# A two-layer metaformer kernel on one core: a new table of numbers for the order of the steps on every engine

## The chip, the cores and the metric

One core of a Trainium2 chip runs the whole program. Its engines are TensorE (PE, the matrix engine, with its weight loads shown as PEld), VectorE (DVE), ScalarE (ACT), GpSimd (POOL) and SyncE (SP, which issues the DMA transfers). The metric is the time of one launch on the device in microseconds. Lower is better.

## What is computed

Thirty-two images of 96 channels and 56 x 56 positions go through two layers. Cut to what matters:

```
# layer 0
x = x + conv0(ln_c(x))      # 1x1 expand 96->576, silu, 3x3 depthwise, silu, squeeze-excite gate,
                            # 1x1 project 576->96, batch norm, + its own input
t = tokens(x); t = t + ffn0(ln_t(t))   # 96->384->96, both products on float8 (5 exponent bits) operands
# layer 1
x = x + conv1(ln_c(x))      # 1x1, group norm over the image, gelu, four shifted copies through two
                            # 1x1 weights, gelu of each, their sum, group norm, 1x1
t = tokens(x); t = t + ffn1(ln_t(t))
```

`ln_c` and `ln_t` normalise each position over its 96 channels. A group norm needs the statistics of a whole image before its first output, and so does the squeeze-excite gate.

## The kernel before

Positions are cut into 8 tiles of 392 (`TW`), numbered 0 to 7. Every stage of an image is a **family** of steps, one per tile (or per chunk of 128 channels and tile), and each engine has its part of a family. The names that the text uses:

- `center_a`, `center 0`, `center 1`, `center 2` and `var ...`: a product that takes the mean off (L523, L598), read by ACT twice (L691 copy, L692 square), then products that sum the squares (L511). `rstd_a`, `rstd 0`, `rstd 1`, `rstd 2` (`seed`, L820) on DVE turn a full set of sums into inverse roots; SP stores them to DRAM and fetches them back broadcast to all channels (`fetch ...`); `norm ...` on DVE multiplies (L842, L901, L906).
- `expand k` (L535, ACT L715), `dw k h j` on DVE: chunk k, half h of the image, tap j of nine, one pass over 128 x 1568 numbers each (L856 for tap 0, L859 for the others); `silu2 k h` on ACT (L742). The last 192 channels go through `texp` (L544, ACT L722) and `tconv` (L557, ACT L733) on PE instead.
- `se1`, `se2`, `se3`: the gate (PE L567, L573; ACT L747, L751; DVE L863 to L871). `proj` (L583, L585) needs it; DVE `x1` (L885) reads it.
- `up`, `quant`, `down`, `add`: the feed-forward blocks, 0 and 1 (PE L618, L627; ACT L775, L782, L789; DVE L914, L921, L924).
- `conv1` (L639, ACT L796), `stats` (L929), `gn 0` (DVE L946 to L966, with two tiny products L646), `gelu1` (ACT L804), `shift` (SP, five DMAs per tile from `g` to `shifted`), `combo` (PE L663, 12 products; ACT three gelus, L810), `fold` (L673, ACT L814), `sum` (DVE L979), `gn 1`, `gn_weights`, `conv3` (L682), `x2` (L983).

The order in which each engine meets its steps is written out by hand: `TIMES` holds for every engine and family one number per step. `timetable` adds 10000 per image, and sorts; an engine then executes its steps in that order. The numbers are keys for the sort alone. No step starts by them: each waits on semaphores for what it needs, and what stands behind a waiting step on its engine waits too. Layer 0 of an image, layer 1 of the image before, and the last feed-forward block of the one before that are in work together, so a steady cycle holds one of each step of all families.

`with_banks` shares three PSUM banks (`ring`, `RING = 3`) among the families of `USES_RING` in the order of PE's steps: a product takes the bank whose last reader has the smallest number, and `wait_bank` makes it wait for that reader. So the numbers of ACT and DVE also decide which bank a product gets.

```
bank = min(free, key=lambda b: free[b])
prev = last[bank]
...
free[bank] = read_at[i, reader]
```

ACT holds one set of function tables at a time. Silu (L715, L722, L733, L742, L747) and gelu (L804, L810) are in different sets, copies and squares in either, so an `ACT_TABLE_LOAD` is put ahead of each first silu after a gelu and the other way round.

Of the kernel before, what the change touches and what calls it, by code (L numbers as in the profile page):

```python
# [47 lines left out]
        "load_x": (1832,), "rstd_a": (4902,), "fetch_a": (4931, 5374, 5857, 5900, 6400, 6627, 6900, 6929),  # L48
        "save_s": (5677, 6677, 6723, 6855, 7082, 7091, 7815, 8098), "texp 0": (8799, 9304, 10303, 10366),
        "texp 1": (11310, 11671, 11721, 12321), "texp 2": (13348, 13418, 13488, 13551),  # L50
        "fetch_s": (17458, 17933, 18453, 18458, 18703, 18742, 19029, 19049), "rstd 0": (20616,),
        "fetch 0": (20784, 20831, 20837, 20843, 21157, 21301, 21302, 21694), "rstd 1": (22328,),
        "fetch 1": (23260, 23290, 23343, 23381, 23422, 23460, 23664, 24595),
        "shift": (24665, 24876, 24982, 25058, 25721, 25722, 26264, 26463), "rstd 2": (28520,),
        "fetch 2": (28558, 28645, 28683, 28721, 29544, 30077, 30293, 30355),
        "store": (30260, 30746, 30809, 30936, 31085, 31161, 31687, 31821)},
# [1145 lines left out]
```

## Time and profile before

| | us |
|---|---|
| runs of the kernel | 6851.56, 6858.68, 6858.77 (median 6858.68) |
| the profiled execution: its time | 6854.27 |
| its span from first to last instruction | 6852.4 |
| busy in it: PE, DVE, ACT, POOL | 5730.9 (84%), 5543.4 (81%), 4409.0 (64%), 452.6 (7%) |
| mean granted TensorE clock (of full speed) | 0.959 |

The times around the span are 1.9 us. The shares are averages over 32 cycles (one for each image in steady work), and a cycle has stretches of different kinds, so a share says little until it is read stretch by stretch.

### The profile page before, as it was taken

The numbers are of one execution on the slowest core, as the hardware profiler recorded it, in microseconds if no ns is written. First come the engines' busy times: TensorE is split into PE (matmuls) and PEld (weight loads), VectorE is DVE, ScalarE is ACT, GpSimd is POOL, SyncE is SP. The second block draws the span as 40 slices with busy tenths as digits, with TensorE's granted clock in tenths as the row PEclk, the third lists the DMA queues.
The fourth block names the chain that finished last, engine by engine and source line by source line (L and its number), as shares of the span: only waits on it lengthen the run. The fifth ranks groups of instructions, "written<-read, shape, count | busy, mean of one in ns | idle before, by whom it ended". The sixth has DMA issues, their size and how long they took to land.

```text
span 6852.4 us, 111430 instructions
## 1 busy us (share of the span) xinstructions
PE 5730.9 (84%) x40192; PEld 2277.5 (33%) x40192; DVE 5543.4 (81%) x9325; ACT 4409.0 (64%) x7671; POOL 452.6 (7%) x366
## 2 busy tenths in 40 slices
PE   2788888888888888888888888888888888888875
PEld 0333333333333333333333333333333333333332
DVE  4788888888888888888888888888888888888863
ACT  1466766666766666766666766666766666766654
POOL 1000000000000000000000000000000000000000
PEclk9899999999999999999999999999999999999997
...
GB/s 41 63 76 86 94 73 86 91 76 85 96 71 85 93 76 85 96 71 87 92 76 85 96 73 86 90 76 84 96 70 85 94 76 84 96 67 88 87 59 62
...
## 3 DMA queue, kind: packets, MB, share of 16 engines
...
## 4 chain that ended last, share of the span: by engine, by line
PE 45%; DVE 31%; ACT 10%; DMA 6%; issue 5%; SPq 4%; DVEq 0%; ACTq 0%; POOL 0%; POOLq 0%
DVE conv L859 16%; PE bank L583 10%; PE bank L598 6%; PE bank L557 4%; PE bank L535 3%; PE bank L585 3%; PE b_banks L682 3%; PE b_banks L639 2%; PE bank L544 2%; DVE hidden L914 2%; PE b_banks L663 2%; ACT hidden L782 2%; PE b_banks L618 2%; DVE xn L906 2%; DVE x L924 2%
## 5 line engine op out<-in xcount | busy, mean ns | idle before, releaser
L859 DVE SCALAR_TENSOR_TENSOR conv<-mid,w_dw,conv 128x1568 f32<-128x1568 f32 x1536 | 2893.7, 1884 | 20.4
L663 PE MATMUL b_banks<-shifted,w_combo 128*32 128x392 f32 x6144 | 681.1, 580 | 311.9 <-DMA shifted<-g 257.8
L535 PE MATMUL bank<-xc_a,w_exp 128*128 128x392 f32 x1536 | 654.9, 525 | 110.1 <-DVE xc_a L842 34.0
L583 PE MATMUL bank<-conv,w_proj_gated 128*96 128x392 f32 x2048 | 728.8, 499 | 4.8 <-DVE x L885 0.5
L598 PE MATMUL bank<-x,centering 128*96 128x392 f32 x1536 | 645.1, 515 | 74.2 <-DVE x L924 39.5
L775 ACT ACTIVATE hidden<-b_banks 128x1176 f16<-128x1176 f32 x512 | 590.0, 1152 | 139.5 <-PE b_banks L618 135.0
L782 ACT ACTIVATE hidden<-hidden 128x1176 fp8e5<-128x1176 f16 x512 | 607.4, 1186 | 39.4 <-DVE hidden L914 39.2
L1001 POOL TENSOR_TENSOR x<-x,xc_a 96x392 f32<-96x392 f32 x256 | 433.2, 1693 | 1729.9 <-DVE xc_a L842 1729.9
L722 ACT ACTIVATE phases<-bank 128x448 f32<-128x448 f32 x384 | 208.5, 543 | 515.5 <-PE bank L544 422.6
L691 ACT ACTIVATE g<-bank 96x392 f32<-96x392 f32 x512 | 256.8, 502 | 337.9 <-PE bank L598 289.6
L618 PE MATMUL b_banks<-xn,w_q 128*128 128x392 fp8e5 x1536 | 348.4, 336 | 133.8 <-ACT hidden L775 116.8
L914 DVE TENSOR_SCALAR hidden<-hidden,b_q 128x392 f16<-128x392 f16 x1536 | 395.0, 313 | 78.4 <-ACT hidden L775 78.0
L663 PEld LDWEIGHTS b_banks<-shifted,w_combo 128*32 128x32 f32 x6144 | 209.5, 123 | 720.6 <-DMA shifted<-g 397.8
L627 PE MATMUL bank<-hidden,w_q 128*96 128x392 fp8e5 x1536 | 356.1, 341 | 93.6 <-ACT hidden L782 54.2
L557 PE MATMUL bank<-phases,w_toeplitz 128*32 128x392 f32 x4608 | 412.4, 495 | 23.4 <-ACT ffn_out L789 22.3
L544 PE MATMUL bank<-xc_a,w_exp 128*32 128x448 f32 x3072 | 381.7, 555 | 58.2 <-ACT phases L722 47.6
L583 PEld LDWEIGHTS bank<-conv,w_proj_gated 128*96 128x96 f32 x2048 | 321.6, 163 | 302.7 <-issue 278.4
L715 ACT ACTIVATE mid<-bank 128x392 f32<-128x392 f32 x768 | 374.6, 501 | 72.9 <-PE bank L535 68.2
L557 PE MATMUL bank<-phases_on,w_toeplitz 128*32 128x392 f32 x4608 | 411.5, 494 | 0.2 <-ACT conv L733 0.2
L691 ACT ACTIVATE xc<-bank 96x392 f32<-96x392 f32 x256 | 125.5, 490 | 434.5 <-PE bank L598 301.9
L733 ACT ACTIVATE conv<-bank,bn_affine 128x392 f32<-128x392 f32 x384 | 258.1, 672 | 201.4 <-PE bank L557 201.4
L535 PEld LDWEIGHTS bank<-xc_a,w_exp 128*128 128x128 f32 x1536 | 259.0, 193 | 377.6 <-issue 245.1
...
## 6 DMA issues: line engine op xcount, KB each, us to landing
...
```

The lines of the kernel that those rows point to most:

```text
L535: mm(ring[bank][:, 0:TW], WEXP[:, 128 * k:128 * k + 128], xc_tile(t, 128), start=True, stop=True)\
L544: last = mm(ring[bank][32 * q:32 * q + 32, 0:EROWS * WW], WEXP[:, m0:m0 + 32], xc_phase(q, h), start=True, stop=True)
L557: last = mm(ring[bank][32 * p:32 * p + 32, 0:TW], TWZ[:, (3 * g + dx) * 2 + r % 2, :], phase_rows(EB if r < 2 else FB, p, QH, dx), start=( ...
L583: mm(o, WPS[:, k, :], tile(conv(k, t // NTH, parity), t % NTH, 128), start=(k == 0), stop=False)
L598: mm(ring[bank][0:C, 0:TW], CEN[:, :], tile(XFULL[1 - parity if L else parity], t, 128), start=True, stop=True)\
L618: last = mm(PB[:, c, 0:TW], W1Q[:, f, 128 * c:128 * c + 128], XN8[t % 2][:, :], start=True, stop=True)
L663: last = mm(rows(PB[32 * u:32 * u + 32, m, 0:TW]), WC[:, u // 2, 32 * m:32 * m + 32], SH[t % 2][:, u, :].rearrange("p (h w) -> p h w", w=G ...
L775: f(Y16[t % 2][:, :, :], PB[:, 0:NHC, 0:TW], ACT.Copy).then_inc(sem["up_evacuated"], 1)
L782: f(Q8[t % 2][:, :, :], Y16[t % 2][:, :, :], ACT.Copy, saturate=False)\
L859: v.scalar_tensor_tensor(out=acc, in0=src, scalar=WDW[:, k, j:j + 1], in1=acc, op0=ALU.mult, op1=ALU.add).then_inc(sem["convolved"], 1)
L914: last = v.tensor_scalar(Y16[t % 2][:, c, :], Y16[t % 2][:, c, :], B1Q[:, g, c:c + 1], 0.0, ALU.add, ALU.max)
L1001: g.tensor_tensor(tile(XA, t), tile(XA, t), xc_tile(t), ALU.add).then_inc(sem["xplus_a"], 1)
```

## The change

Every number of `TIMES` is replaced; nothing else is. The numbers of the instructions of each kind stay the same, except the table loads of ACT, which follow from the order. Two lines of the table:

```diff
-        "silu2 0": (9468, 11523), "expand 1": (9508, 9893, 9929, 10551, 10751, 11101, 11648, 11677),
+        "silu2 0": (9013, 13806), "expand 1": (9372, 9530, 10080, 10510, 10723, 10860, 11304, 11409),
```

The order that follows, at three places of a steady cycle.

ACT, from the load ahead of `combo 4` of the kernel before (and `combo 3` of the changed one) to the last silu of layer 0's convolution, `silu2 2 1` (L742). L810 are the gelus of a tile, L814 is `fold`, L715 is `expand 0`. Before:

```order
L810 ACT_TABLE_LOAD
L810 ACTIVATE gelus<-b_banks 128x392 x3
L814 ACTIVATE g<-bank 96x392
L810 ACTIVATE hidden<-b_banks 128x392 x3
L814 ACTIVATE g<-bank 96x392
L715 ACT_TABLE_LOAD
L715 ACTIVATE mid<-bank 128x7x56
L814 ACTIVATE g<-bank 96x392
L742 ACTIVATE conv,pool_sums<-conv,bn_affine 128x1568
```

The same engine and place in the changed kernel:

```order
L810 ACT_TABLE_LOAD
L810 ACTIVATE hidden<-b_banks 128x392 x3
L810 ACTIVATE gelus<-b_banks 128x392 x3
L814 ACTIVATE g<-bank 96x392
L715 ACT_TABLE_LOAD
L715 ACTIVATE mid<-bank 128x7x56
L814 ACTIVATE g<-bank 96x392
L810 ACT_TABLE_LOAD
L810 ACTIVATE hidden<-b_banks 128x392 x3
L715 ACT_TABLE_LOAD
L715 ACTIVATE mid<-bank 128x7x56
L742 ACTIVATE conv,pool_sums<-conv,bn_affine 128x1568
```

`silu2 2 0`, which stood behind `combo 3`, now stands ahead of it (just above the second list's first row). A second `expand 0` step has moved ahead of `silu2 2 1`, with a table load of its own and one for the gelus before it. Over the program ACT has 371 table loads in place of 311, or 12 in place of 10 in a cycle.

DVE, the last steps ahead of `gn 0` (L946 is its first instruction). L929 is `stats`, L901 `norm 1`, L856 and L859 are the convolution passes `dw 2 0`. Before:

```order
L859 SCALAR_TENSOR_TENSOR conv<-mid,w_dw,conv 128x1568
L929 BN_STATS bn_stats<-g 96x6
L856 TENSOR_SCALAR conv<-mid,w_dw 128x1568
L901 TENSOR_TENSOR g<-g,r_b 96x392 x2
L859 SCALAR_TENSOR_TENSOR conv<-mid,w_dw,conv 128x1568
L929 BN_STATS bn_stats<-g 96x6 x4
L946 BN_AGGR gn_small<-bn_stats 96x2
```

The changed kernel:

```order
L856 TENSOR_SCALAR conv<-mid,w_dw 128x1568
L901 TENSOR_TENSOR g<-g,r_b 96x392
L859 SCALAR_TENSOR_TENSOR conv<-mid,w_dw,conv 128x1568
L929 BN_STATS bn_stats<-g 96x6
L901 TENSOR_TENSOR g<-g,r_b 96x392
L929 BN_STATS bn_stats<-g 96x6
L859 SCALAR_TENSOR_TENSOR conv<-mid,w_dw,conv 128x1568
L929 BN_STATS bn_stats<-g 96x6 x3
L946 BN_AGGR gn_small<-bn_stats 96x2
```

One pass more (L859, `dw 2 0 2`) now stands ahead of `gn 0`; behind it, ahead of `rstd_a`, two passes stand where there were three. In the same way `rstd 0` now has the pass `dw 0 1 3` behind it that stood ahead of it, and `rstd 1` has `dw 1 0 8` and `dw 1 1 0` ahead of it that stood behind.

PE, ahead of `proj 7`, the last projection tile of an image (L583, L585). L627 is `down 1`, L618 `up 1`, L598 `center 0`, L511 `var 0`. Before:

```order
L627 MATMUL bank<-hidden,w_q 96x392 x3
L511 MATMUL sums_a<-sq_a,row_select 32x98 x4
L598 MATMUL bank<-x,centering 96x392
L627 MATMUL bank<-hidden,w_q 96x392 x3
L618 MATMUL b_banks<-xn_0,w_q 128x392 x3
L511 MATMUL sums_a<-sq_a,row_select 32x98 x4
L583 MATMUL bank<-conv_2,w_proj_gated 96x392
L583 MATMUL bank<-conv,w_proj_gated 96x392 x3
L585 MATMUL bank<-conv,w_proj_gated 96x392
```

The changed kernel:

```order
L627 MATMUL bank<-hidden,w_q 96x392 x3
L618 MATMUL b_banks<-xn_0,w_q 128x392 x3
L598 MATMUL bank<-x,centering 96x392
L511 MATMUL sums_a<-sq_a,row_select 32x98 x8
L583 MATMUL bank<-conv_2,w_proj_gated 96x392
L583 MATMUL bank<-conv,w_proj_gated 96x392 x3
L585 MATMUL bank<-conv,w_proj_gated 96x392
L627 MATMUL bank<-hidden,w_q 96x392 x3
L544 MATMUL bank<-xc_a,w_exp 32x448 x4
```

`down 1 1`, `center 0 6` and `var 0 5` have moved from ahead of `proj 7` to behind it. Earlier in the same stretch `conv3 0` and `conv3 1` now stand ahead of `proj 1`, where both stood behind it. On ACT, `silu2 0 1` has moved from among the steps of `quant 0` and `down 0` to the `texp 2` steps that follow that block, and `tconv 0 2` and `tconv 0 3` from between `quant 1` steps to behind `down 1 7` and `up 0 3`.

## Rows read from the trace of the kernel before

**Rows 1.** `se2` on DVE (L863): count, shortest/median/longest in ns, first and last start.

```profile
L863 DVE TENSOR_TENSOR gate<-bank,b_se x32: 142/165/166, 254.3 to 6604.8; 128x5 f32<-128x5 f32 x32
```

**Rows 2.** Busy time by engine in five stretches of one cycle.

```profile
core 0: us, PE busy (x) PEld busy (x) DVE busy (x) ACT busy (x) POOL busy (x), PEclk, DMA share, GB/s
3277.57:3324.10 46.53, 34.83 (x312) 13.11 (x313) 37.67 (x48) 36.50 (x59) 12.65 (x7) 0.93 0.59 143
3324.10:3379.34 55.24, 54.30 (x269) 22.96 (x268) 36.70 (x73) 22.01 (x42) 1.01 (x1) 1.00 0.20 57
3379.34:3389.14 9.80, 7.74 (x55) 3.44 (x53) 9.38 (x13) 8.18 (x12) 0.00 (x0) 1.00 0.25 59
3389.14:3472.25 83.11, 72.89 (x556) 27.71 (x556) 79.23 (x137) 62.60 (x114) 0.30 (x3) 1.00 0.30 78
3472.25:3482.45 10.20, 5.85 (x68) 2.74 (x68) 8.59 (x23) 8.70 (x17) 0.00 (x0) 1.00 0.21 44
```

**Rows 3.** Timeline, ACT, around `silu2 2 1`: start, us, [idle before, what ended it].

```profile
3291.81 0.50 ACT L810 ACTIVATE gelus<-b_banks 128x392 f32<-128x392 f32 x1 [0.16 <-PE b_banks L663]
...
3304.73 1.28 ACT L715 ACT_TABLE_LOAD   x1
3306.03 0.50 ACT L715 ACTIVATE mid<-bank 128x392 f32<-128x392 f32 x1
...
3307.43 1.69 ACT L742 ACTIVATE conv<-conv,bn_affine 128x1568 f32<-128x1568 f32 x1 [0.52 <-DVE conv L859]
...
3318.69 0.21 ACT L751 ACTIVATE gate<-gate 128x5 f32<-128x5 f32 x1
```

**Rows 4.** Timeline, DVE, two short steps, and a pass of tap 0 (L856).

```profile
3303.03 4.36 DVE L859 SCALAR_TENSOR_TENSOR conv<-mid,w_dw,conv 128x1568 f32<-128x1568 f32 x2
3307.32 0.55 DVE L842 TENSOR_TENSOR xc_a<-xc_a,r_a 96x392 f32<-96x392 f32 x1
3307.79 0.55 DVE L979 BATCH_NORM_STATS2 bn_stats<-g 96x6 f32<-96x392 f32 x1
...
3380.79 1.03 DVE L856 TENSOR_SCALAR conv<-mid,w_dw 128x1568 f32<-128x1568 f32 x1
```

**Rows 5.** Timeline, PE, ahead of `proj 7`.

```profile
3373.20 0.90 PE L598 MATMUL bank<-x,centering 128*96 128x392 f32 x2
3374.10 0.70 PE L627 MATMUL bank<-hidden,w_q 128*96 128x392 fp8e5 x3
...
3375.22 0.38 PE L511 MATMUL sums_a<-sq_a,row_select 128*32 128x98 f32 x8
```

**Rows 6.** A wait of PE in the second stretch: total, times, longest.

```profile
PE bank L598 <- DVE x L983: 0.7, 1, 0.7
```

**Rows 7.** The three longest waits of DVE in the fourth stretch.

```profile
DVE var_b L827 <- PE sums_b L511: 0.7, 1, 0.7
DVE xn L906 <- PE b_banks L618: 0.6, 1, 0.6
DVE g L901 <- DMA r_b<-rstd_row_b: 0.5, 1, 0.5
```

**Rows 8.** Busy time from `rstd 0` to `rstd 1`, in the columns of rows 2.

```profile
3389.14:3440.30 51.16, 43.59 (x321) 18.13 (x322) 48.57 (x96) 46.92 (x80) 0.00 (x0) 1.00 0.32 86
```

**Rows 9.** Timeline, ACT, inside that stretch.

```profile
3392.28 1.15 ACT L775 ACTIVATE hidden<-b_banks 128x1176 f16<-128x1176 f32 x1 [1.19 <-PE b_banks L618]
...
3417.57 1.70 ACT L742 ACTIVATE conv<-conv,bn_affine 128x1568 f32<-128x1568 f32 x1
```

**Rows 10.** Timeline, DVE, from `gn 0` to the passes behind it.

```profile
3472.25 0.37 DVE L946 BATCH_NORM_AGGREGATE gn_small<-bn_stats 96x2 f32<-96x48 f32 x1
...
3476.91 5.61 DVE L859 SCALAR_TENSOR_TENSOR conv<-mid,w_dw,conv 128x1568 f32<-128x1568 f32 x3
```

**Rows 11.** Timeline, PE, the last `var_a` and the first `combo`.

```profile
3480.96 0.38 PE L511 MATMUL sums_a<-sq_a,row_select 128*32 128x98 f32 x8 [0.39 <-ACT sq_a L692]
3483.94 2.80 PE L663 MATMUL b_banks<-shifted,w_combo 128*32 128x392 f32 x16 [2.60 <-DMA shifted<-g]
```

**Rows 12.** Table loads ahead of L810: count, busy us, mean ns, idle before.

```profile
L810 ACT ACT_TABLE_LOAD x124 | 159.1, 1283 | 7.8 <-PE b_banks L663 5.3
```

More of the change, by code:

```diff
@@ L47 @@
     "SP": {
[L48 to L56, printed above, removed]
-    "PE": {
-        "center_a": (2930, 3375, 3666, 3845, 3961, 3995, 3996, 4332),
-        "var_a": (3849, 3859, 3904, 4073, 4097, 4335, 4336, 4364),
[14 rows of a table removed]
-        "combo": (24379, 24390, 24475, 24764, 25147, 25452, 25664, 26125),
[6 rows of a table removed]
@@ L81 @@
-    "ACT": {
-        "center_a": (3485, 3805, 3930, 4351, 4378, 4548, 4596, 4650),
[13 rows of a table removed]
-        "combo": (25176, 25335, 25376, 25414, 25883, 26039, 26540, 26805),
-        "fold": (25278, 25839, 25946, 26117, 26395, 26634, 27208, 27210),
[4 rows of a table removed]
-    "DVE": {
-        "rstd_a": (4562,), "norm_a": (4688, 5183, 5364, 5669, 5951, 6083, 6315, 6746),
[17 rows of a table removed]
+        "load_x": (2344,), "rstd_a": (5345,), "fetch_a": (5366, 5656, 5858, 6242, 6983, 7247, 7377, 7900),
+        "save_s": (7699, 7737, 7972, 8044, 8090, 8333, 8657, 8694), "texp 0": (10321, 10373, 10445, 11000),
@@ new lines @@
+        "texp 1": (11573, 11980, 12385, 12514), "texp 2": (13382, 13434, 14072, 14386),
+        "fetch_s": (18152, 18675, 18992, 19218, 19512, 19641, 19847, 20320), "rstd 0": (20669,),
+        "fetch 0": (21042, 21074, 21452, 21487, 21518, 21984, 22014, 22129), "rstd 1": (23168,),
+        "fetch 1": (23285, 23298, 23380, 23757, 24322, 24376, 24397, 24567),
+        "shift": (25024, 25215, 25391, 25601, 25754, 26249, 26546, 27195), "rstd 2": (29200,),
+        "fetch 2": (29220, 29315, 29580, 29957, 30065, 30345, 30364, 30535),
@@ new lines @@
+        "store": (30488, 31249, 31283, 31451, 31660, 31685, 31872, 32128)},
+    "PE": {
+        "center_a": (3136, 3234, 3430, 3612, 3784, 3947, 4050, 4072),
+        "var_a": (3519, 3543, 3686, 4205, 4211, 4374, 4493, 4592),
[14 rows of a table added]
+        "combo": (24608, 24745, 24931, 25159, 25299, 25520, 25707, 26156),
[6 rows of a table added]
+    "ACT": {
+        "center_a": (4281, 4339, 4375, 4551, 4588, 4711, 4756, 4787),
[13 rows of a table added]
+        "combo": (25221, 25279, 25345, 25734, 25782, 26226, 26358, 26522),
+        "fold": (25268, 25333, 25564, 25823, 26213, 26348, 26697, 26815),
[4 rows of a table added]
@@ L121 @@
+    "DVE": {
+        "rstd_a": (4322,), "norm_a": (4521, 5040, 5684, 5689, 6214, 6444, 6750, 6933),
[17 rows of a table added]
     "POOL": {
-        "norm_a": (12718, 12775, 12862, 12887, 12912, 13053, 16342, 17167), "gn 0": (27816,)},
+        "norm_a": (10579, 11625, 11923, 15434, 16177, 16347, 17018, 17886), "gn 0": (30050,)},
 }
```

106 rows, old and new, of the table TIMES are left out of this document.

## Prediction

> **What bounds the kernel now.** The page's shares (PE 84%, DVE 81%) name no bound, so I read the length of a cycle first, then one cycle by stretches, then what waits at each joint. The gate's DVE step starts 32 times, first at 254.3 us and last at 6604.8 us [rows 1]: a cycle is 6350.5 / 31 = 204.85 us, and 31 cycles are 93% of the time. What the order changes in a cycle is worth 31 times.
>
> The joints of one cycle are `rstd_a`, `proj 0`, the DVE step `x1 7`, `rstd 0`, `gn 0`, and `rstd_a` again. Between them [rows 2] the reader sees two different kernels. In stretch B (`proj 0` to `x1 7`, 55.24 us) PE is busy 54.30 us and DVE 36.70. In D (`rstd 0` to `gn 0`, 83.11 us) DVE is busy 79.23 us and PE 72.89. C (9.80 us) and E (10.20) belong to DVE too. A (46.53 us) begins with the last passes on DVE, and its second half is the gate's chain: last pass, `silu2 2 1` on ACT, `se1`, `se2`, `se3`, and beside it the last `combo` and `fold`, which end in `gn 1` and then `proj 0`. From the silu at 3307.43 to the gate's tanh at 3318.69 [rows 3] ACT takes 11.26 us. So the chain is DVE from `x1 7` to the last pass, then ACT and small steps, then PE alone. I cost the change stretch by stretch on that chain.
>
> **A, `rstd_a` to `proj 0`.** The new order puts one `norm_a` and one `sum` ahead of the last pass; they follow each other at 0.48 us [rows 4], so the pass ends 0.95 us later. ACT must have got to the silu by then. It now has `silu2 2 0`, two more table loads and one more `expand 0` ahead of it. From the last gelu of `combo 2` to that silu ACT will do five loads (1.3 each with the gap behind it, 6.5), `silu2 2 0` (1.7), three gelu triples (1.28 each, 3.8), two expands (1.0) and three folds (some 0.47 each, as an expand of 0.50 with its overlap; 1.4): 14.4 us, by the durations of [rows 3]. That last gelu ends at 3292.31, 14.7 us after `rstd_a`; as it hangs on `gn 0`, and E below is 0.95 us shorter, it will be 15.7. ACT is there at 30.1. The pass ended when the silu began, at 3307.4 [rows 3], and will end at 29.85 + 0.95 = 30.8. It fits, by 0.7 us. Behind the silu a table load and an `expand 0` are gone (1.28 + 0.5 us [rows 3]); a load moves from an `expand` to `se1`, which costs nothing in sum. That is -1.8. Then `expand 0 6` (0.8 us, as a pair of products on PE) stands between `gn 1` and `proj 0`: +0.8. A: +0.95 - 1.8 + 0.8, so 0.
>
> What a table load costs is the row to watch here. A load takes 1283 ns, and 124 of them had 7.8 us of idle time ahead of them [rows 12]; the activation behind the load of 3304.73 starts at 3306.03, 0.02 us after the load's end [rows 3]. So a load costs 1.3 us. The two more in a cycle are 2.6 us of ACT's work, which lie beside DVE's passes, and on the chain if the 0.7 us above isn't there. The Trainium skill's page "ScalarE: Activation LUTs", section "What ACT_TABLE_LOAD costs", puts a drain of about 1.38 us on top, 2.66 us for every switch of set. By that rule ACT would reach the silu 2.8 us later than I have it, and the sum below would be +0.9 us a cycle where it is -1.15. The trace doesn't agree: no such drain stands between load and activation.
>
> **B, `proj 0` to `x1 7`.** Three steps leave it for a place behind `proj 7`: a `center` product pair (0.90 us), a `down` (0.70) and a `var` (0.38) [rows 5]. They overlap their neighbours by some 0.2 us in sum, which leaves 1.75. PE's wait of 0.7 us for `x2` [rows 6] should mostly go as well, since `conv3 0` no longer stands behind `proj 1` and DVE has `x2 0` done a projection earlier. I take 0.45 of it. B: -2.2.
>
> **C, `x1 7` to `rstd 0`.** DVE has less to do here than before (`dw 0 1 3` went behind `rstd 0`, `dw 0 1 0` ahead of `x1 7`), so the end is that of `var 0 7`. From the end of `proj 7` its chain is the first `down`, then ACT's down copy, `texp`, quant, up copy, expand, center, up copy, expand, center one behind the other, then `var`. Those are eleven instructions on ACT at 46.92 / 80 = 0.59 us [rows 8], 6.5 in sum; with the first `down` (0.70), the last `var` (0.38 [rows 5]) and four handovers between PE and ACT, for which I allow 0.35 us each, it is 9.0 us behind `proj 7`, 8.8 behind `x1 7`. C: -1.0.
>
> **D, `rstd 0` to `gn 0`.** Two passes come in, `dw 0 1 3` and `dw 2 0 2`, each 5.61 / 3 = 1.87 us [rows 10], and one `norm 2` step, of the 0.48 of the short steps [rows 4]: +4.2. What they may give back are DVE's waits, of which the three longest are 1.8 us [rows 7] and all of them 2.5. ACT is the engine that feeds DVE here. From `rstd 0` to `rstd 1` it is busy 46.92 of 51.16 us [rows 8], more than in any other stretch. It loses `silu2 0 1` (1.8 us with its read, 1.70 of it in [rows 9]) and gains a quant and a down copy, which I put at 1.6 (a 128 x 1176 step is 1.15 [rows 9], a tile of 392 about 0.5 [rows 3]), while DVE's part grows by 5.25 (the first pass, the `norm`, `dw 1 0 8`, and the 1.03 us [rows 4] of `dw 1 1 0`). I keep 1.3 us of waits. D: +4.2 - 1.2 = +3.0.
>
> **E, `gn 0` to `rstd_a`.** One pass leaves: -1.87. But `rstd_a` needs the last `var_a`, which ended at 3480.96 + 0.38 = 3481.34, 9.1 us after `gn 0` [rows 10, 11], and that chain (`gn 0`, first gelu, three centers on ACT, squares summed) keeps its order. So DVE now waits about 0.9 us there, a new wait. E: -0.95.
>
> **The sum.** 0 - 2.2 - 1.0 + 3.0 - 0.95 = -1.15 us a cycle, 31 times -36 us. The profiled execution took 6854.3 us: 6818.6. It is 4.4 us below the median of the runs: 6823. The start (254 us) and the last image's end (248 us) I leave as they are; they have the same steps with more room.
>
> **Rivals.**
>
> 1. More comes than that. The waits of D go altogether (-1.3 against my value), B gives the 0.7 us in full and C and E do as said with DVE alone as their limit (-0.5 and -0.3 more): about -3.3 a cycle, 6854 - 102 + 4 = 6757. For it speaks that every handover from PE or ACT to DVE in D now has more passes around it. Against it is that ACT is as full as [rows 8] show.
>
> 2. No change. Each engine's work stays, and gains in B and C come back as waits of DVE further on: within 0.2% (13.7 us, about what a measurement of this kernel can tell from no change), 6859.
>
> 3. Slower by the banks. ACT now reads `tconv 0 2` and `tconv 0 3` late, so two of the three ring banks are held, and `expand 1 3`, `texp 1 0`, `texp 1 1`, `down 1 7`, `expand 1 4` and `texp 1 2` take the third in turn, each behind its predecessor's read. The nearest row is ACT's wait for a late product, 1.19 us [rows 9]; six of them are 7.2 us of idle time on ACT. Its stretch can hide 51.16 + 5.25 - 1.3 - 46.7 - 4.2 = 4.2, and 3 us would be late at `rstd 1`: -1.15 + 3 = +1.85 a cycle, 6859 + 57 = 6916. It decides from 5.4 us on. For it speaks the order alone; against it, that ACT has other steps of over 1 us between most of the six.
>
> 4. Slower by the gelus. `gn 0` stands a pass later, so the gelus, the shifts and the combos start later against DVE, and PE already waits 2.60 us for the first shifted tile [rows 11]. If transfers or the loads make ACT late at `silu2 2 1`, the two loads (2.6 us) are on the chain in full: +1.45 a cycle, 6904. It decides from 0.7 + 1.15 = 1.9 us of lateness on.
>
> **How the numbers follow.** My case 0.48 (its own range 6800 to 6845, from the two ends of D's waits, 0 and 2.5, and half a microsecond for C), rival 1 0.16, rival 2 0.14, rival 3 0.12, rival 4 0.10. I predict 6823. The range leaves out the far half of rival 1 and what rivals 3 and 4 give beyond 6895, under 2 in 10 together: 6765 to 6895. Faster by over 0.2% has my case and rival 1, 0.64; within 0.2% 0.15; slower 0.21.
>
> **What would show it.** In the profile after: a cycle by L863 of about 203.7 us; `proj 0` to `x1 7` about 53 us with PE still over 97% busy; a wait of DVE L827 for PE's `sums_a` of about 0.9 us once a cycle, which before didn't exist; ACT's last silu still released by DVE's pass, not late behind a load; `rstd 0` to `gn 0` about 86 us. I am wrong if ACT is the one that is waited for in D, with idle time of its own behind single bank trips (rival 3), or if the silu starts right behind its `expand` with no idle time (rival 4).

## The result, and the profile after

| us | before | changed |
|---|---|---|
| median of the runs | 6855.12 (6844.88 to 6858.77, 4 runs) | 6778.85 (6770.24 to 6788.07, 4 runs) |
| ratio, with its 95% interval | | 0.9891 [0.9873, 0.991] |
| the profiled execution: time, span | 6854.27, 6852.4 | 6775.25, 6773.4 |
| busy in it: PE, DVE, ACT, POOL | 5730.9, 5543.4, 4409.0, 452.6 | 5680.4, 5500.9, 4490.3, 514.3 |

The changed kernel is faster by 76 us, or by 79 between the two profiled executions; 36 were forecast. The sign and the range held, the size did not: it is more than twice the forecast.

A cycle first, as in [rows 1]. `se2` of the changed kernel, with its 32 starts:

```profile
L863 DVE TENSOR_TENSOR gate<-bank,b_se x32: 164/165/165, 253.0 to 6531.4; 128x5 f32<-128x5 f32 x32
```

(6531.4 - 253.0) / 31 = 202.53 us where it was 204.85: -2.32 a cycle, 72 of the 79 us. (The first of the 31 cycles is 4.3 us longer than before, so those in the middle differ by more than 2.32.) Then the five stretches of one undisturbed cycle, cut at the same joints as [rows 2]. Columns are PE, PEld, DVE, ACT, POOL busy, PEclk, DMA share and GB/s:

```profile
3043.32:3089.49 46.17, 34.64 (x312) 13.29 (x313) 37.41 (x51) 39.89 (x61) 14.67 (x7) 0.93 0.61 144
3089.49:3142.66 53.17, 53.17 (x264) 22.52 (x262) 36.13 (x69) 20.99 (x40) 1.00 (x1) 1.00 0.22 60
3142.66:3150.12 7.46, 6.41 (x55) 2.45 (x48) 6.79 (x13) 6.82 (x12) 0.00 (x0) 1.00 0.29 70
3150.12:3235.88 85.76, 75.13 (x575) 28.90 (x573) 83.12 (x138) 65.35 (x117) 0.30 (x3) 1.00 0.31 78
3235.88:3245.21 9.33, 5.97 (x68) 2.68 (x60) 6.83 (x21) 7.76 (x15) 0.00 (x0) 0.95 0.16 33
```

The reader is to see that in the second row PE is busy for the whole stretch: its idle time between `proj 0` and `x1 7` is gone. The third row is 2.3 us shorter than before, the fourth 2.7 longer, with DVE busy 97% of it.

Single cycles differ, so what follows uses means. Each is the mean, over 23 cycles in the middle of the program, of the time between the starts of the same two instructions in the trace:

| mean of 23 cycles, us | before | changed | difference | forecast |
|---|---|---|---|---|
| A, `rstd_a` to `proj 0` | 47.29 | 47.18 | -0.1 | 0 |
| B, `proj 0` to `x1 7` | 55.34 | 53.17 | -2.2 | -2.2 |
| C, `x1 7` to `rstd 0` | 9.45 | 7.46 | -2.0 | -1.0 |
| D, `rstd 0` to `gn 0` | 83.43 | 85.97 | +2.5 | +3.0 |
| E, `gn 0` to `rstd_a` | 10.23 | 9.22 | -1.0 | -0.95 |
| a cycle | 205.75 | 203.00 | -2.75 | -1.15 |
| inside B and C: `proj 0` to `proj 7` | 51.53 | 48.41 | -3.1 | |
| inside B and C: `proj 7` to the start of `var 0 7` | 11.84 | 11.72 | -0.1 | |
| inside B and C: the start of `var 0 7` to `rstd 0` | 1.41 | 0.50 | -0.9 | |

B met its forecast by chance. PE reached `proj 7` 3.1 us earlier, but `x1 7` stood 0.95 us later behind `proj 7` than before, because DVE now had `dw 0 1 0` (L856) ahead of it, and that pass overwrites a buffer which `proj 7` still reads. A wait of DVE in B that the rows before don't have:

```profile
DVE conv L856 <- PE bank L585: 2.5, 1, 2.5
```

What C gained beyond its forecast is this same 0.95, given back: `proj 7` to `rstd 0` went from 13.26 to 12.22 us, the -1.0 of the forecast. So B and C are read together from here on: forecast -3.2, measured -4.16, and the difference lies ahead of `proj 7`.

The place of [rows 3], ACT around `silu2 2 1`, in the changed kernel:

```profile
3069.73 1.28 ACT L810 ACT_TABLE_LOAD   x1 [0.41 <-PE b_banks L663]
3071.03 1.27 ACT L810 ACTIVATE hidden<-b_banks 128x392 f32<-128x392 f32 x3
3072.32 1.28 ACT L715 ACT_TABLE_LOAD   x1
3073.61 0.50 ACT L715 ACTIVATE mid<-bank 128x392 f32<-128x392 f32 x1
3074.12 1.70 ACT L742 ACTIVATE conv<-conv,bn_affine 128x1568 f32<-128x1568 f32 x1
...
3083.57 0.21 ACT L751 ACTIVATE gate<-gate 128x5 f32<-128x5 f32 x1
```

and the pass it needs, on DVE:

```profile
3069.72 4.36 DVE L859 SCALAR_TENSOR_TENSOR conv<-mid,w_dw,conv 128x1568 f32<-128x1568 f32 x2
```

From silu to tanh it is 9.45 us where it was 11.26, the -1.8 of the forecast. The pass ends at 3074.08, and ACT is ready at 3074.11. The 0.7 us by which ACT was to be early are not there, so the two table loads of this place fit with nothing to spare. Over the 23 cycles the silu starts 0.27 us behind the pass's end in the mean (0.07 before) and 1.07 at the most, and in 11 of them ACT comes to it straight from its `expand` with no idle time. The activation of 3071.03 starts 0.02 us after its load's end, as before.

### The profile page after: what moved, and what is told of

Its sections match the earlier page's. It is cut to its first block, busy times and chain, and to the rows that moved or that the text cites. A ratio compares the mean times of both kernels' runs of the same rounds, so it can differ in the third digit from the quotient of the medians.

```text
span 6773.4 us, 111490 instructions
## 1 busy us (share of the span) xinstructions
PE 5680.4 (84%) x40192; PEld 2257.1 (33%) x40192; DVE 5500.9 (81%) x9325; ACT 4490.3 (66%) x7731; POOL 514.3 (8%) x366
## 4 chain that ended last, share of the span: by engine, by line
PE 46%; DVE 24%; ACT 13%; issue 7%; SPq 5%; DMA 5%; ACTq 0%; DVEq 0%
DVE conv L859 12%; PE bank L583 10%; PE bank L598 7%; PE bank L557 6%; PE bank L535 4%; PE bank L585 3%; PE b_banks L682 3%; DVE hidden L914 3%; PE bank L544 2%; DVE xn L906 2%; PE b_banks L639 2%; ACT hidden L782 2%; PE b_banks L618 1%; PE sums_b L511 1%; PE b_banks L663 1%
## 5 line engine op out<-in xcount | busy, mean ns | idle before, releaser
L859 DVE SCALAR_TENSOR_TENSOR conv<-mid,w_dw,conv 128x1568 f32<-128x1568 f32 x1536 | 2883.1, 1877 | 17.2
L535 PE MATMUL bank<-xc_a,w_exp 128*128 128x392 f32 x1536 | 688.6, 534 | 195.7 <-DVE xc_a L842 78.1
L583 PE MATMUL bank<-conv,w_proj_gated 128*96 128x392 f32 x2048 | 728.2, 498 | 0.0
L598 PE MATMUL bank<-x,centering 128*96 128x392 f32 x1536 | 638.0, 510 | 32.8 <-ACT mid L715 15.8
L1001 POOL TENSOR_TENSOR x<-x,xc_a 96x392 f32<-96x392 f32 x256 | 494.8, 1937 | 1635.6 <-DVE xc_a L842 1635.6
L715 ACT ACTIVATE mid<-bank 128x392 f32<-128x392 f32 x768 | 381.7, 503 | 160.2 <-PE bank L535 157.8
L583 PEld LDWEIGHTS bank<-conv,w_proj_gated 128*96 128x96 f32 x2048 | 320.7, 163 | 340.8 <-issue 319.9
L618 PE MATMUL b_banks<-xn,w_q 128*128 128x392 fp8e5 x1536 | 346.1, 335 | 99.9 <-DVE xn L906 61.2
L535 PEld LDWEIGHTS bank<-xc_a,w_exp 128*128 128x128 f32 x1536 | 243.5, 191 | 552.9 <-issue 374.8
L544 PE MATMUL bank<-xc_a,w_exp 128*32 128x448 f32 x3072 | 372.1, 551 | 56.7 <-ACT phases L722 33.6
L742 ACT ACTIVATE conv<-conv,bn_affine 128x1568 f32<-128x1568 f32 x192 | 326.4, 1700 | 121.3 <-DVE conv L859 120.1
L663 PEld LDWEIGHTS b_banks<-shifted,w_combo 128*32 128x32 f32 x6144 | 225.8, 118 | 525.7 <-issue 256.7
L789 ACT ACTIVATE ffn_out<-bank 96x392 f16<-96x392 f32 x512 | 253.4, 495 | 200.8 <-PE bank L627 189.3
L627 PE MATMUL bank<-hidden,w_q 128*96 128x392 fp8e5 x1536 | 348.5, 339 | 27.1 <-ACT phases L722 19.8
```

The source lines that it names most:

```text
L535: mm(ring[bank][:, 0:TW], WEXP[:, 128 * k:128 * k + 128], xc_tile(t, 128), start=True, stop=True)\
L544: last = mm(ring[bank][32 * q:32 * q + 32, 0:EROWS * WW], WEXP[:, m0:m0 + 32], xc_phase(q, h), start=True, stop=True)
L583: mm(o, WPS[:, k, :], tile(conv(k, t // NTH, parity), t % NTH, 128), start=(k == 0), stop=False)
L598: mm(ring[bank][0:C, 0:TW], CEN[:, :], tile(XFULL[1 - parity if L else parity], t, 128), start=True, stop=True)\
L618: last = mm(PB[:, c, 0:TW], W1Q[:, f, 128 * c:128 * c + 128], XN8[t % 2][:, :], start=True, stop=True)
L663: last = mm(rows(PB[32 * u:32 * u + 32, m, 0:TW]), WC[:, u // 2, 32 * m:32 * m + 32], SH[t % 2][:, u, :].rearrange("p (h w) -> p h w", w=G ...
```

## The experiments

In the diffs a family's numbers are those of its steps 0, 1, 2 and so on. Each ratio is against runs of the kernel before taken with it, whose median lay between 6841 and 6860 us, so ratios are compared here and not times. The changed kernel stands at 0.9891 [0.9873, 0.991] and "no change" at 1; 0.01 is 2.2 us a cycle. Where I give a cycle or a stretch, it is the mean of 23 cycles as above.

### Parts taken back out of the changed kernel

**x1_proj7_back.** `down 1 1`, `center 0 6` and `var 0 5` ahead of `proj 7` again on PE.

```diff
-        "center 0": (17134, 18375, 18799, 18972, 18998, 19340, 19710, 19841),
-        "var 0": (18334, 18762, 19075, 19527, 19575, 19759, 19832, 19942),
+        "center 0": (17134, 18375, 18799, 18972, 18998, 19340, 19580, 19841),
+        "var 0": (18334, 18762, 19075, 19527, 19575, 19590, 19832, 19942),
...
-        "down 1": (29198, 29600, 30006, 30158, 30339, 30550, 30551, 30725)},
+        "down 1": (29198, 29585, 30006, 30158, 30339, 30550, 30551, 30725)},
```

> The changed kernel with three PE steps (down 1 1, center 0 6, var 0 5) put back ahead of proj 7, and nothing else. Chain theory: the stretch from proj 0 to proj 7 is PE alone, so the 1.75 us of these steps come back in each cycle, 31 x 1.75 = 54 us: about 6833 us against 6779 for the changed kernel (ratio to before 0.997), and rstd 0 later by the same 1.75 us behind proj 0. Rival (the gain came from steadier transfers and other waits of DVE, with PE's order of no weight): within 10 us of 6779, ratio 0.989.

Measured: 6822.15 us, 0.9944 [0.993, 0.9959]. `proj 7` started 1.65 us later, for which the prediction had 1.75. Behind it `var 0 7` came 0.8 us sooner, so that B and C together lost 0.95; A was 0.7 longer, on which more below. The price of the three steps on PE was right; nearly half of it is given back at once behind `proj 7`.

**x2_conv3_back.** `conv3 0` and `conv3 1` behind `proj 1` on PE, as before.

```diff
-        "se2": (16230,), "proj": (16648, 16832, 18646, 18744, 18841, 19119, 19189, 19597),
+        "se2": (16230,), "proj": (16648, 16668, 18646, 18744, 18841, 19119, 19189, 19597),
```

> The changed kernel with proj 1 put back ahead of texp 0 1, conv3 0 and conv3 1 on PE. Chain theory: the stretch proj 0 to proj 7 had no PE wait at all in the changed kernel, and the wait for x2 (0.7 us in the kernel before) returns: +0.7 to +1.0 us a cycle, 6779 + 22 to 31 = 6801 to 6810 us (ratio 0.992 to 0.993). Rival (this order is of no weight, since center 2 0 is now further behind conv3 0): 6779 within 7 us.

Measured: 6827.05 us, 0.9978 [0.9968, 0.9987]. `proj 0` to `proj 7` took 50.19 us in place of 48.41, +1.8. This edit costs more than the 0.45 at which the prediction valued its opposite, and more than the 0.7 to 1.0 expected of the run. The waits of PE from `proj 0` to `x1 7` were none in the changed kernel, and here:

```profile
PE bank L598 <- DVE x L885: 1.7, 1, 1.7
```

PE's product `center 2 0` takes the bank of `proj 0` and waits for its reader, `x1 0`: DVE in the new order has `x2 0` and `x2 1` ahead of it, and these need `conv3 0` and `conv3 1`, which stand later on PE now. The wait is of another kind than that of [rows 6], and larger.

**x3_pass_behind_gn0.** `dw 2 0 2` behind `gn 0` again on DVE.

```diff
-        "dw 2 0": (13499, 13710, 13874, 14124, 14291, 14342, 14418, 14495, 14604),
+        "dw 2 0": (13499, 13710, 14080, 14124, 14291, 14342, 14418, 14495, 14604),
```

> The changed kernel with the DVE pass dw 2 0 2 put back behind gn 0. Chain theory: rstd 0 to gn 0 loses 1.87 us, gn 0 to rstd_a gains 1.0, since the wait of 0.89 us of rstd_a for the last var_a goes and 0.98 us of the pass stand open: -0.9 us a cycle, 6779 - 27 = 6752 us (ratio 0.985). Rival (the later pass gave the chain conv1, stats, gn 0 the time that it needs, so DVE waits for ACT at stats instead): the wait of DVE for L796 grows from 0.4 us to over 1.3 us a cycle, and the time is 6779 within 5 us.

Measured: 6803.25 us, 0.992 [0.9903, 0.9936]. The rival was right on the waits; of its time ("within 5 us") that can't be said, as the ratio is 0.003 above the changed kernel's, with intervals that overlap. `rstd 1` to `gn 0` stayed at 30.68 us (30.69 in the changed kernel) with a pass of 1.87 us less in it, and DVE waited for ACT instead:

```profile
DVE bn_stats L929 <- ACT g L796: 1.4, 2, 1.0
```

E grew from 9.22 to 10.13, and its wait of L827 was gone; A was 0.3 shorter. So what ends at `gn 0` in x3 is the chain norm, `conv1`, ACT copy, `stats`; the pass that the change moved there cost nothing, where the prediction charged 1.87.

**x4_silu_back.** ACT's `silu2 0 1` among the steps of `quant 0` again.

```diff
-        "silu2 0": (9013, 13806), "expand 1": (9372, 9530, 10080, 10510, 10723, 10860, 11304, 11409),
+        "silu2 0": (9013, 11230), "expand 1": (9372, 9530, 10080, 10510, 10723, 10860, 11304, 11409),
```

> The changed kernel with ACT's silu2 0 1 (1.8 us with its read) back among the steps of quant 0 and down 0 between rstd 0 and rstd 1, where the kernel before had it. By the prediction's account of D ACT is nearly as full there as DVE, so 1.8 us more on it would be late in part: about +0.5 to +1.0 us a cycle, ratio 0.991 to 0.994. If D is DVE's passes and ACT has 7.7 us of idle time between rstd 0 and rstd 1 that can take it (as its waits in the changed kernel say), nothing: 0.989. I lean to the first, since the waits of ACT there are short ones between steps that others need.

Measured: 6817.54 us, 0.9947 [0.9934, 0.9959]. `rstd 0` to `rstd 1` went from 55.28 to 56.49 us, `rstd 1` to `gn 0` from 30.69 to 30.29: +0.8 in D, of 1.9 us of ACT's work. ACT feeds DVE there as the prediction argued, and the silu's leaving is what paid for part of the passes.

**x8_tconv_back.** ACT reads `tconv 0 2` and `tconv 0 3` early again.

```diff
-        "tconv 0": (10335, 10350, 10663, 10814), "texp 1": (10560, 10643, 10895, 10936),
+        "tconv 0": (10335, 10350, 10355, 10440), "texp 1": (10560, 10643, 10895, 10936),
```

> The changed kernel with ACT's tconv 0 2 and tconv 0 3 put back among the quant 1 steps, so that their two ring banks come free early. Chain theory: ACT's idle time from rstd 0 to rstd 1 (7.7 us against 4.5 in the kernel before) falls by 1 us or more, and is hidden by DVE's passes anyway: 6779 within 7 us (ratio 0.989). Rival (waits for banks hold up the feed-forward block and so rstd 1): faster, -1 us a cycle, about 6748 us (ratio 0.984).

Measured: 6854.69 us, 1.0024 [1.0014, 1.0033]. Neither theory had this: one move of two reads takes back more than the whole gain. `rstd 0` to `rstd 1` is 58.02 us where it was 55.28. ACT's waits there in one cycle:

```profile
ACT ffn_out L789 <- PE bank L627: 3.1, 3, 2.2
ACT conv L733 <- PE bank L557: 2.9, 2, 2.1
ACT g L691 <- PE bank L598: 2.6, 1, 2.6
```

In the changed kernel the row of L733 does not exist in this stretch. ACT now stands at `tconv 0 2` before PE has made it, with a quant and an up copy behind it, for which DVE then waits:

```profile
DVE hidden L914 <- ACT hidden L775: 2.9, 4, 1.1
```

**x14_three_ahead_of_var.** On PE `down 1 2`, `up 1 5` and `expand 1 2` ahead of `var 0 7`, as in the kernel before, and their reads on ACT moved alike.

```diff
-        "expand 1": (9679, 9755, 10040, 10569, 11158, 11213, 11307, 11434),
+        "expand 1": (9679, 9755, 9862, 10569, 11158, 11213, 11307, 11434),
...
-        "up 1": (28888, 29112, 29310, 29647, 29734, 30075, 30214, 30340),
-        "down 1": (29198, 29600, 30006, 30158, 30339, 30550, 30551, 30725)},
+        "up 1": (28888, 29112, 29310, 29647, 29734, 29860, 30214, 30340),
+        "down 1": (29198, 29600, 29850, 30158, 30339, 30550, 30551, 30725)},
```

> The changed kernel with PE's down 1 2, up 1 5 and expand 1 2 back ahead of var 0 7, and their reads on ACT moved alike. Theory (these steps are the part of C that the prediction missed): var 0 7 starts 1.9 us later or more (0.70 + 0.67 + 0.82 less the overlaps, and PE's wait for the up copy of 1.3 us comes back), rstd 0 with it, and D gives back less than half since its own chain starts with them: 1.0 to 2.0 us a cycle slower, ratio 0.994 to 0.999. Rival (C is held by ACT's chain alone, as the prediction had it): var 0 7 unchanged, ratio 0.989.

Measured: 6832.77 us, 0.9965 [0.9956, 0.9974], +2.04 us a cycle: `var 0 7` 0.92 later, D +0.7, A +0.45. The end of PE's list behind `proj 7`, in the changed kernel

```profile
3147.67 0.90 PE L598 MATMUL bank<-x,centering 128*96 128x392 f32 x2
3149.62 0.38 PE L511 MATMUL sums_a<-sq_a,row_select 128*32 128x98 f32 x8 [1.05 <-ACT sq_a L692]
```

and in this run:

```profile
3174.86 0.90 PE L598 MATMUL bank<-x,centering 128*96 128x392 f32 x2
3175.65 0.70 PE L627 MATMUL bank<-hidden,w_q 128*96 128x392 fp8e5 x3
3176.19 0.66 PE L618 MATMUL b_banks<-xn,w_q 128*128 128x392 fp8e5 x3
3176.90 0.90 PE L535 MATMUL bank<-xc_a,w_exp 128*128 128x392 f32 x2
3177.72 0.38 PE L511 MATMUL sums_a<-sq_a,row_select 128*32 128x98 f32 x8
```

In the first PE waits 1.05 us for ACT's last square: ACT's chain is the limit, as the prediction had it. In the second three products fill that gap and 0.92 more, and PE is the limit. The prediction never counted these three.

### Parts put into the kernel before

**x5_only_proj.** PE's moves around `proj 7` and `conv3` alone.

```diff
-        "center 0": (17920, 18618, 18664, 18783, 19245, 19269, 19345, 19725),
-        "var 0": (18224, 18950, 19026, 19276, 19320, 19439, 19788, 20048),
+        "center 0": (17920, 18618, 18664, 18783, 19245, 19269, 19483, 19725),
+        "var 0": (18224, 18950, 19026, 19276, 19320, 19484, 19788, 20048),
...
-        "conv3": (27269, 27378, 27421, 27431, 27445, 27554, 27627, 27656),
+        "conv3": (27240, 27242, 27421, 27431, 27445, 27554, 27627, 27656),
...
-        "down 1": (29306, 29371, 29844, 30061, 30210, 30287, 30534, 30893)},
+        "down 1": (29306, 29482, 29844, 30061, 30210, 30287, 30534, 30893)},
```

> The kernel before with the PE part of the change around the projections alone: down 1 1, center 0 6 and var 0 5 behind proj 7, conv3 0 and conv3 1 ahead of proj 1. Chain theory: proj 0 to proj 7 falls from 51.5 us by 1.75 for the steps and by up to 1.0 for PE's waits there, and DVE, which waited 1.3 us for proj 7 and 17 us in the whole stretch, can follow: -2.0 to -2.7 us a cycle, 6855 - 62 to 84 = 6771 to 6793 us (ratio 0.988 to 0.991), nearly all of the change's gain. Rival (what PE saves comes back as waits of DVE or of the bank ring further on, and the gain needs the new order of DVE and ACT too): -1 us a cycle or less, 6824 us or more (ratio over 0.9955).

Measured: 6958.57 us, 1.0146 [1.013, 1.0161]: slower. `proj 7` started some 1.6 us earlier, but from `proj 7` to `var 0 7` it took 16.83 us in place of 11.84. ACT's own order still had the copy of `down 1 1` ahead of the up and quant steps, so it stood still for it:

```profile
ACT ffn_out L789 <- PE bank L627: 4.1, 2, 3.6
```

**x9_proj_and_readers.** The same with the readers moved alike.

```diff
# on top of x5: ACT, ACT, DVE
-        "center 0": (18314, 18522, 18606, 18654, 18957, 19185, 19453, 19722),
-        "down 1": (29201, 29327, 29696, 29841, 30089, 30260, 30503, 30688)},
-        "add 1": (29194, 29242, 30058, 30155, 30192, 30802, 30858, 31244)},
+        "center 0": (18314, 18522, 18606, 18654, 18957, 19185, 19482, 19722),
+        "down 1": (29201, 29480, 29696, 29841, 30089, 30260, 30503, 30688)},
+        "add 1": (29194, 29330, 30058, 30155, 30192, 30802, 30858, 31244)},
```

> The kernel before with PE's part around the projections as in x5, and with the readers moved along: ACT's down 1 1 and center 0 6 behind quant 1 2, and DVE's add 1 1 behind x1 7. Chain theory: x5 lost because ACT stood at down 1 1, which PE now gave it only behind proj 7, with up 1 2 and quant 1 2 behind it; with the readers moved that wait goes, and -2 us a cycle is left, 6855 - 62 = 6793 us (ratio 0.991). Rival (the rest of the order of DVE or the banks eat it as well): 6824 us or more (ratio over 0.9955).

Measured: 6831.93 us, 0.9986 [0.9976, 0.9995]. x5's loss is gone, but hardly any gain is left: `proj 0` to `proj 7` -1.6, `proj 7` to `var 0 7` +1.5. The -1.6 is the price of the three steps and no more. PE still sat idle for 1.26 us of `proj 0` to `proj 7` (1.02 before), though `conv3 0` and `conv3 1` stand ahead of `proj 1` here; its wait for `x2` had become one for ACT:

```profile
PE bank L598 <- ACT phases L722: 0.8, 1, 0.8
```

So the place of `conv3` on PE is worth nothing without the changed orders of DVE and ACT behind it.

**x10_b_and_c.** On top of x9, `silu2 0 0` on ACT and `dw 0 1 3` on DVE leave C.

```diff
-        "silu2 0": (9468, 11523), "expand 1": (9508, 9893, 9929, 10551, 10751, 11101, 11648, 11677),
+        "silu2 0": (9900, 11523), "expand 1": (9508, 9893, 9929, 10551, 10751, 11101, 11648, 11677),
...
-        "dw 0 1": (9411, 9665, 9728, 9762, 10489, 10889, 11068, 11263, 11389),
+        "dw 0 1": (9411, 9665, 9728, 9820, 10489, 10889, 11068, 11263, 11389),
```

> The kernel before with the steps around proj 7 and conv3 of the run x9 (which left 0.9986), and two more moves of the change: on ACT silu2 0 0, which stood right behind proj 7 in the chain that ends in var 0 7 (1.70 + 0.2 us), goes behind that chain, and on DVE dw 0 1 3 goes behind rstd 0. Theory (the change's gain in B and C is the three steps and the two seams off PE, and it can only be kept if ACT's silu and DVE's pass leave C as well): proj 7 to rstd 0 falls from 15.1 us in x9 to about 13.0 or below, proj 0 to rstd 0 to about 62.5, D pays some 1.5 of the 1.84 us pass; a cycle 1.0 to 1.5 us shorter than in x9, ratio 0.991 to 0.994. Rival (C is held by ACT's quant and up copies alone, or D gives everything back): the ratio stays at 0.998 to 1.000.

Measured: 6857.69 us, 1.0007 [0.9998, 1.0016]; the rival. `proj 0` to `rstd 0` was 63.82 us (before 64.79), D 84.67 (before 83.43): what B and C won, D took back. From `proj 7` to `var 0 7` it was 13.37 us still, with 15 steps of PE (the last `var` among them) where the changed kernel has 12.

**x13_b_and_c_full.** On top of x10, `down 1 2`, `up 1 5` and `expand 1 2` of PE and their reads on ACT go behind `var 0 7`.

```diff
-        "expand 1": (9717, 9794, 10020, 10610, 10846, 11218, 11556, 11586),
+        "expand 1": (9717, 9794, 10052, 10610, 10846, 11218, 11556, 11586),
...
-        "up 1": (28932, 29089, 29395, 29645, 29904, 29955, 30150, 30276),
-        "down 1": (29306, 29482, 29844, 30061, 30210, 30287, 30534, 30893)},
+        "up 1": (28932, 29089, 29395, 29645, 29904, 30050, 30150, 30276),
+        "down 1": (29306, 29482, 30049, 30061, 30210, 30287, 30534, 30893)},
...
-        "up 1": (28783, 28817, 29461, 29488, 29721, 29760, 29974, 30095),
-        "down 1": (29201, 29480, 29696, 29841, 30089, 30260, 30503, 30688)},
+        "up 1": (28783, 28817, 29461, 29488, 29721, 29897, 29974, 30095),
+        "down 1": (29201, 29480, 29895, 29941, 30089, 30260, 30503, 30688)},
```

(ACT's `center 0 7` also went ahead of `up 1 4`.)

> The kernel before with the moves of x10 and three more, which the prediction did not see: PE's down 1 2, up 1 5 and expand 1 2 go from ahead of var 0 7 to behind it (0.70, 0.67 and 0.82 us), with ACT's readers moved alike and center 0 7 ahead of up 1 4. In x10 proj 7 to var 0 7 took 13.4 us, in the changed kernel 11.7. Theory (the missing part of B and C is these three steps): proj 7 to var 0 7 about 11.7 to 12.3, proj 0 to rstd 0 about 62.0, and D, which gets them, takes back at most half of it: ratio 0.993 to 0.997. Rival (D of the order before gives everything back, since its feed-forward chain is as tight as in x10, where 1.0 us won in B and C came back as 1.2 in D): 0.999 to 1.003. I lean to the rival: every part of the order put alone into the kernel before has given nothing so far.

Measured: 6854.89 us, 1.0 [0.9992, 1.0009]. `proj 7` to `var 0 7` fell from 13.37 to 11.28 us, below the changed kernel's 11.72: these three steps are what x10 lacked. But `rstd 0` followed only 2.2 us later, since DVE wasn't there, and D was 84.93. One cycle from `proj 0` on:

```profile
3119.41:3172.99 53.58, 52.35 (x255) 22.48 (x255) 35.74 (x70) 19.29 (x37) 1.01 (x1) 1.00 0.21 57
3172.99:3182.73 9.74, 8.73 (x65) 3.81 (x63) 8.49 (x14) 7.56 (x13) 0.00 (x0) 1.00 0.28 72
3182.73:3267.56 84.83, 73.74 (x560) 27.89 (x559) 81.00 (x138) 65.66 (x118) 0.30 (x3) 1.00 0.31 76
```

PE has 1.2 us of idle time in B, where the changed kernel has none.

**x11_tconv_late.** ACT alone reads `tconv 0 2` and `tconv 0 3` late, rival 3's mechanism without the rest of the change. The two reads stand a few steps earlier than in the changed kernel. Seven ring products of a cycle then wait for another reader than before (three of them take another bank).

```diff
-        "tconv 0": (10085, 10155, 10238, 10511), "texp 1": (10563, 10604, 10929, 10941),
+        "tconv 0": (10085, 10155, 10625, 10680), "texp 1": (10563, 10604, 10929, 10941),
```

> The kernel before with one part of the change on ACT alone: the reads of tconv 0 2 and tconv 0 3 go from between quant 1 steps to behind quant 0 0 and up 0 2, so that two of the three ring banks are held longer and seven products take other banks. Rival 3 of the prediction (the steps on the third bank wait for each other): up to 3 us a cycle slower at rstd 1, ratio up to 1.014. Theory that the read's place is a gain in itself (as the run x8 could be read, where putting it early again cost 1.35%): ratio 0.987. Theory that the read only has to stand behind PE's own place for the product, which in the kernel before it does: 1.000 to 1.003. I expect the last.

Measured: 6943.49 us, 1.0135 [1.0121, 1.0149], +2.6 us a cycle, of which 2.4 between `rstd 0` and `rstd 1`. I expected 1.000 to 1.003, and the rival's "up to 1.014" is what came. PE waits for ACT's late reads (L733) at L544 and L627, 1.5 us a cycle over the program, where it was 0.0 before. One cycle has these two, and DVE's wait of [rows 7] for PE's `up` product, grown from 0.6:

```profile
PE bank L544 <- ACT conv L733: 0.8, 1, 0.8
PE bank L627 <- ACT conv L733: 0.7, 1, 0.7
DVE xn L906 <- PE b_banks L618: 2.7, 2, 2.5
```

### Table loads and the last pass

**x6_two_loads_less.** `expand 0 0` earlier on ACT, so that 10 loads stand in a cycle, not 12.

```diff
-        "expand 0": (6082, 6293, 6407, 6734, 6829, 6892, 7231, 8106), "texp 0": (7084, 7567, 9180, 9992),
+        "expand 0": (5350, 6293, 6407, 6734, 6829, 6892, 7231, 8106), "texp 0": (7084, 7567, 9180, 9992),
```

> The changed kernel with one ACT step, expand 0 0, moved ahead of fold 2, right behind silu2 2 0, which takes two table loads (2.6 us) out of a cycle, 10 in place of 12, all ahead of silu2 2 1. Chain theory: ACT has slack there and the last silu waits for DVE's pass, so the time stays, 6779 within 7 us (ratio 0.989), and ACT's idle time ahead of that silu grows. Rival (table loads are on the chain): up to -2.6 us a cycle, 6698 to 6740 us (ratio 0.977 to 0.983).

Measured: 6785.3 us, 0.9895 [0.988, 0.9909], as the changed kernel. The two loads are off the chain: ACT's idle time ahead of the last silu grew from 0.10 to 0.68 us in the mean, and the silu's 0.2 us of lateness stayed.

**x7_pass_before_rstd_a.** One more pass, `dw 2 0 5`, ahead of `rstd_a`, into DVE's new wait of E, and the first `norm_a` a pass later.

```diff
-        "rstd_a": (4322,), "norm_a": (4521, 5040, 5684, 5689, 6214, 6444, 6750, 6933),
+        "rstd_a": (4322,), "norm_a": (4610, 5040, 5684, 5689, 6214, 6444, 6750, 6933),
...
-        "dw 2 0": (13499, 13710, 13874, 14124, 14291, 14342, 14418, 14495, 14604),
+        "dw 2 0": (13499, 13710, 13874, 14124, 14291, 14315, 14418, 14495, 14604),
```

> The changed kernel with the DVE pass dw 2 0 5 moved ahead of rstd_a, into its wait of 0.89 us for the last var_a, and norm_a 0 moved behind dw 2 0 8, so that as many passes as before cover the fetch. Chain theory: the last pass of the chunk ends 0.9 us earlier against gn 0, and with it the last silu, the gate and proj 0: -0.9 us a cycle, 6779 - 27 = 6752 us (ratio 0.985). Rival (behind gn 0 the chain of gelus, shifts and combos is the later one by now, since it hangs on gn 0 and not on DVE's passes): the last silu waits for ACT's own work, 6779 within 7 us or above.

Measured: 6752.78 us, 0.9875 [0.9854, 0.9895]. The interval overlaps the changed kernel's, so a gain isn't shown by the runs; the medians would give 0.35 us a cycle. In its profiled execution, the fastest of its four, a cycle is 202.14 us, 0.86 less, but the last silu stands only 0.43 us earlier behind `gn 0`, where the pass stands 1.47 earlier. Here ACT is late, as rival 4 had it. DVE's last pass, and ACT at the same place:

```profile
3044.82 4.36 DVE L859 SCALAR_TENSOR_TENSOR conv<-mid,w_dw,conv 128x1568 f32<-128x1568 f32 x2
```

```profile
3048.49 1.28 ACT L715 ACT_TABLE_LOAD   x1
3049.78 0.50 ACT L715 ACTIVATE mid<-bank 128x392 f32<-128x392 f32 x1
3050.18 1.68 ACT L742 ACTIVATE conv<-conv,bn_affine 128x1568 f32<-128x1568 f32 x1
```

The pass ends at 3049.18 and the silu starts at 3050.18, with no idle time of ACT before it: 1.0 us late behind a load and an `expand`, and 1.3 in the mean of the 23 cycles.

**x12_both.** x7 and x6 together.

> The changed kernel with the two edits that did no harm by themselves put together: the last pass of DVE ahead of rstd_a with its norm_a behind it (x7: 0.9875) and expand 0 0 earlier on ACT so that two table loads of a cycle fall away (x6: 0.9895, as the changed kernel's 0.9891). If the loads are off the chain in x7 as well, the ratio is that of x7, 0.986 to 0.988. If x7's shorter stretch has made ACT the one that is late at silu2 2 1, the loads are worth something now: 0.983 to 0.985.

Measured: 6736.85 us, 0.9831 [0.9818, 0.9845], the fastest of all, and in the band given for "the loads are worth something now". The pass and the silu of one cycle:

```profile
3040.78 4.37 DVE L859 SCALAR_TENSOR_TENSOR conv<-mid,w_dw,conv 128x1568 f32<-128x1568 f32 x2
```

```profile
3045.44 1.68 ACT L742 ACTIVATE conv<-conv,bn_affine 128x1568 f32<-128x1568 f32 x1
```

ACT is 0.29 us late and no longer 1.0 (0.44 and 1.31 in the means). The same two loads that x6 took away for nothing are now worth the step from 0.9875 to 0.9831, whose intervals are apart.

## Why the prediction was right in part, and which step failed

**The step that failed** is in B: "I take 0.45 of it", what the prediction gave for PE's own waits between `proj 0` and `proj 7` beside the three steps. It measured 1.5, with all of PE's idle time gone, and it hangs on the new orders of DVE and ACT and not on `conv3`'s place alone (x2, x9). Of the 1.6 us by which a cycle gained more than forecast, this is 1.0, and D is 0.5.

**What bounds the kernel** held for B (PE alone), for D and E (DVE), and for ACT's silu in the middle of A. C belonged to DVE before, which came 0.9 us late to `rstd 0`; in the changed kernel it ends with `var 0 7`, as forecast.

**A** (forecast 0). The two parts came as worked out: silu to tanh -1.8, `gn 1` to `proj 0` +0.8 (1.70 to 2.51 us). Only the margin was wrong, 0.0 us instead of 0.7. The last gelu of `combo 2` ended 15.0 us after `rstd_a` (15.7 forecast), but from there to the silu it took 15.8 us and not 14.4: the sum had ACT's work and no waits, and ACT waits for PE's `combo` and `fold` products between (0.41 us in the timeline above). That cost some 0.2 us a cycle here. A load costs 1.3 us and no more. By the Trainium skill's "ScalarE: Activation LUTs", "What ACT_TABLE_LOAD costs", with its drain behind every load, ACT would have reached the silu 2.8 us later than the prediction had it; it came 0.7 later, by the waits, and no drain stands behind a load in the trace (0.02 us).

**B and C** (forecast -3.2, measured -4.16). The three steps were priced rightly (x1: 1.65 for 1.75). PE's idle time between `proj 0` and `proj 7` was 1.0 us a cycle, more than the wait of 0.7 in [rows 6], and all of it went. `proj 0` to `proj 7` shrank by 3.1: 1.65 of it the three steps, and about 1.5 the place of `conv3` together with the readers' order around it (x2 puts 1.8 on it). The reason given, that `conv3 0` no longer stands behind `proj 1`, is only half of it: in x9, where that is so without the new orders of DVE and ACT, PE's waits stay. The rest of the difference to PE's waits, some 0.4, I can't place. In C, that `var 0 7` would stand at the end of ACT's chain was right: PE waits 1.05 us for it, and from the end of `proj 7` (3140.70 + 0.90) to the last `var` at 3149.62 it is 8.0 us, 8.4 with the `var` itself, where 9.0 were forecast. But PE would have been the limit if three products (`down 1 2`, `up 1 5`, `expand 1 2`) had not left as well, which the prediction did not list. With them back C is 0.9 us longer (x14). `silu2 0 0` left too.

**D** (forecast +3.0, measured +2.5). The two parts of the sum came about as forecast, DVE's busy time +3.8 for +4.2 and its idle time -1.2 for -1.2 (means of the 23 cycles). Their places did not. The pass `dw 2 0 2` was charged with 1.87 and cost nothing (x3): it fills DVE's waits for ACT ahead of `gn 0`. Of the 5.25 us added ahead of `rstd 1` 3.8 stayed in the length of `rstd 0` to `rstd 1`, and the silu's leaving is worth 0.8 of what was given back (x4).

**E** (forecast -0.95, measured -1.0) held with its mechanism, DVE's new wait for `sums_a`, 0.9 us a cycle; in the cycle above:

```profile
DVE var_a L827 <- PE sums_a L511: 1.0, 1, 1.0
```

Before and in x3 and x7 it is 0.0.

**The rivals.** The result lies between my case and rival 1, whose reason for B (the wait goes in full) is what happened. (Rival 1's terms add up to -3.5 a cycle, not -3.3.) Rival 3 named a real mechanism with about the right price: in x11 it costs 2.4 us at `rstd 1`. In the changed kernel no product of PE waits for a read of L733. That this is because PE's own `tconv` steps moved too is argued from x8, where with the reads early again ACT is the one that waits. Rival 4's sign, a silu right behind its `expand`, is there in 11 of 23 cycles, at 0.2 us a cycle and not the 1.9 from which it decides, and the 0.2 us stayed in x6 with two loads less. One pass earlier the sign is there in all 23 (x7).

**What no single part shows.** x9, x10 and x13 put ever more of B and C into the kernel before and gained next to nothing: 0.9986, 1.0007, 1.0. x13 has as few steps of PE between `proj 7` and `var 0 7` as the changed kernel, but its DVE wasn't ready at `rstd 0`, PE idled 1.2 us in B, and D took back 1.5 us. Yet each of x1, x2, x4, x8 and x14 loses part of the gain when one move is taken out of the whole. The losses don't add up to the gain (by the ratios 1.2, 1.9, 1.2, 2.9 and 1.6 us a cycle against 2.4), so they are not independent shares; which further moves of D make it bear the added passes was not separated and stays open.
